# Four tokens to a partition, a second layer one step behind, and scatters two experts behind

## The chip, the core and the metric

The kernel runs on one core of a Trainium2 chip. The core has a matrix engine (TensorE, PE in the profile, with PEld for its weight loads), three other compute engines (VectorE or DVE, ScalarE or ACT, GpSimd or POOL), a queue engine (SyncE or SP) and 16 DMA engines. The metric is the device time of one execution in microseconds (us); lower is better.

## The reference

```python
x = x + xattn(ctx_512, layernorm(x), W0, ..., b0, W1, ..., b1)     # two graph attention layers
x = x + ffn(layernorm(x), gate_w, gate_up_proj, down_proj, shared_gate_w, shared_up_w, shared_down_w)

def gat_layer(x, adj, W, a_self, a_neigh, b):
    feat = einsum('nf,hfo->hno', x, W)
    e = leaky_relu(attn_self[:, :, None] + attn_neigh[:, None, :])
    e = e + MASK_VAL * (1.0 - adj)[None, :, :]                      # adj is layernorm(x)
    out = einsum('hnm,hmo->hno', softmax(e), feat) + b[:, None, :]
    return elu(out)

def ffn(x, ...):                                                    # 64 experts, 6 a token, 128 slots
    scores = softmax(xf @ gate_w.T); topk_w, topk_idx = top_k(scores, 6)
    hid = silu(g) * u; eo = (hid @ down_proj) * weight              # for each expert, on its tokens
    return scatter_add(eo) + silu(xf @ shared_gate_w.T) * (xf @ shared_up_w.T) @ shared_down_w.T
```

x is 4 batches of 512 tokens of 512 numbers, the context 4 x 512 x 128. All is float32. The mask term is so large that each token attends to one node only, the one with the largest layernorm value. So the kernel computes an attention layer as product, bias and elu on all nodes, and applies the two attention steps as one lookup: node of node, then a gather of feature rows. A flag worked out from bounds on the inputs sends other inputs to a general path, which does not run here.

## The kernel before

Token n of a batch sits in partition n % 128 of tile n // 128: 4 tiles of 128 tokens to a batch, 16 in all.

**The first stretch** is a loop over 16 steps, one for each tile (n = 4b + t). On PE a step holds one column block of the first layer of the next batch (`first_layer`, L577), the four products of the second layer of this tile (`second_layer`, L587) and two transposes of shared weights in steps 4 to 11 (`weight_turn`, L560), which start only when all four loads of `raw_in` have landed. ACT and DVE follow in the same order. On DVE a step also holds `elu2` of the tile before (L992) and the search for the largest x (`largest`). SP stores each feature tile to DRAM (`store_feat`, L302). POOL stores the four node columns of a batch (`store_node`, L402, 4 bytes to a descriptor), looks up node of node (L408), gathers the feature rows (`pick`, L420), adds them to x (`add`, L429) and finishes the scale of the normalisation (`scale`). DVE takes the moments in `moments` (L1026), and ACT writes the normalised rows (`norm`, L856: it reads x with a step of four numbers and writes runs). PE transposes them (`xn_turn`, L567).

**The second stretch** is the routing of the four batches, in an order written out by hand on each engine: gate product (`gate`, L601: the tokens are the standing operand, the 64 gate columns stream), choice of six (`choose`), positions in the experts (`place`), one-hot columns (`split`, DVE), and products that turn them into a list of tokens for each expert (`invert`, `collect`). Ten units of the shared part of batch 0 lie in between or behind: `half_up` is units 0 to 5 (L664) and `shared_down` units 6 to 9 (L678). Six of them stand between the routing steps and four behind the last of them. ACT takes part with `silu` (L881), which waits for a unit.

**The third stretch** is the loop over 64 experts. PE: the product with `gu_w` (L785), the transposes of the next expert's gathered rows (L765), a unit of the shared part in some steps (30 units over 52 experts), the product with `dn_w` of the expert before (L773). DVE scales the result into one of `YB` = 8 buffers y (L1215). POOL runs one queue in this order:

```python
for e in range(E):
    scatter(e, 0)
    scatter(e, 1)
    if e + GX < E:
        gather(e + GX)
    if e + 1 < E and shared_before(e + 1) > shared_before(e):
        for h in range(2):
            pool.wait_ge(half_added[h], 16 * (e + 1))
        add_shared(shared_before(e + 1))
```

`scatter(e, h)` (L507) adds half of every row to the output in DRAM. It waits for y of expert e and for the landing of the same half of expert e - 1, so the 64 scatters of a half are a chain. `gather(e)` (L514) fills one of `GX` = 6 buffers and waits for y of expert e - 6. `add_shared` (L498) adds a batch's shared part to the output. It comes behind the scatters of experts 19, 36 and 53, waits until they have landed, and the next scatter waits for it.

Of the kernel before, what the change touches and what calls it, by code (L numbers as in the profile page):

```python
# [37 lines left out]
YB = 8  # L38
EXP_FLOOR = -87.336
# [27 lines left out]
def allocate(nc, ctx, k):  # L67
# [14 lines left out]
    k.eighth = sb("eighth", [P, P], F16)  # L82
    k.pick_a = sb("pick_a", [P, (2 * SLO - 1) * SHI], F16)
# [7 lines left out]
def main_block(nc, k, a):  # L91
# [3 lines left out]
    with ExitStack() as ctx:  # L95
# [7 lines left out]
        with ExitStack() as early:  # L103
            def er(name, shape, dt=F32):
                return early.enter_context(nc.sbuf_tensor(name, shape, dt))

            gate_raw = er("gate_raw", [E, D])
            raw = er("raw", [P, 2 * SC, D])
            raw_down = er("raw_down", [P, KC, SI])
            absw = er("absw", [P, KC + 1, H * O], F16)  # L110
            square = er("square", [P, 2, D], F16)
# [22 lines left out]
        spare2 = sb("spare2", [P, E])  # L134
        sg = sb("sg", [P, 2, N])
# [3 lines left out]
        with ExitStack() as first:  # L139
# [4 lines left out]
            w1 = at("w1", [P, KC, H * O])  # L144
# [14 lines left out]
            at("behind_nodes", [P, 3, 256])  # L159
# [23 lines left out]
            wts = at("wts", [P, 2, TB, E])  # L183
# [16 lines left out]
        w0_in, b0_in, small_in, w1_in, raw_in = (sem(s) for s in ("w0_in", "b0_in", "small_in", "w1_in", "raw_in"))  # L200
# [3 lines left out]
        node_stored = [sem(f"node_stored{j}") for j in range(2)]  # L204
# [60 lines left out]
        order += [("xn", n) for n in range(NT)]  # L265
# [19 lines left out]

        ahead = [4, 6, 8, 9, 10, 11, 12, 13, 14, 15, 16] + [NT] * 6

        with nc.Block() as block:
            @block.sync
            def _(sp):  # L290
                def load_nodes(b):
                    sp.dma_start(nodes[:, b * TB:(b + 1) * TB, :],
                                 a["ctx"][b * N:(b + 1) * N, :].rearrange("(t p) f -> p t f", p=P)).then_inc(nodes_in[b], 16)
# [5 lines left out]
                def store_feat(b):  # L299
                    for t in range(TB):  # L300
                        sp.wait_ge(z2_ready, b * TB + t + 1)
                        sp.dma_start(a[f"feat_dram{b}"][t * P:(t + 1) * P, :], feat[:, t, :]).then_inc(feat_out[t], 16)  # L302

                def store_x2(b):
                    sp.wait_ge(x2_ready, (b + 1) * TB)
                    sp.dma_start(a["out"][b * N:(b + 1) * N, :].rearrange("(t p) d -> p t d", p=P),
                                 k.x[:, b * TB:(b + 1) * TB, :]).then_inc(x2_out, 16)

                def load_expert(e):
# [4 lines left out]
                    for j in range(2):  # L314
# [4 lines left out]
                             a["W0"].rearrange("h f o -> f h o")).then_inc(w0_in, 16)  # L319
                load_nodes(1)  # L320
                load_x(0)
                for c in range(KC):
                    sp.dma_start(w1[:, c, :].rearrange("f (h o) -> f h o", h=H),
                                 a["W1"][:, c * P:(c + 1) * P, :].rearrange("h f o -> f h o")).then_inc(w1_in, 16)
                sp.dma_start(b1bc[:], a["b1"].rearrange("h o -> (h o)").rearrange("(u d) -> u d", u=1)
                             .broadcast_to([P, H * O])).then_inc(w1_in, 16)
                load_x(1)
                load_nodes(2)
                load_x(2)
                load_nodes(3)  # L330
                sp.dma_start(gate_raw[:], a["gate_w"]).then_inc(raw_in, 16)
                load_x(3)
                sp.dma_start(raw[:, 0:SC, :], a["sh_gate"].rearrange("(s p) d -> p s d", p=P)).then_inc(raw_in, 16)
                sp.dma_start(raw[:, SC:2 * SC, :], a["sh_up"].rearrange("(s p) d -> p s d", p=P)).then_inc(raw_in, 16)
                sp.dma_start(raw_down[:], a["sh_down"].rearrange("(c p) s -> p c s", p=P)).then_inc(raw_in, 16)
                for j, name in enumerate(("a_self0", "a_neigh0", "a_self1", "a_neigh1", "b0")):
                    sp.dma_start(small[:, j, :], a[name]).then_inc(small_in, 16)
                store_feat(0)
                store_feat(1)
                store_feat(2)  # L340
                store_feat(3)
# [13 lines left out]
                sp.dma_start(a["out"][0:N, :].rearrange("(t p) d -> p t d", p=P), k.x[:, 0:TB, :]).then_inc(x3_out, 16)  # L355
# [5 lines left out]
            def _(pool):  # L361
                counted = [0]

                def count(ins):
# [11 lines left out]
                nc.gpsimd.iota(token_i[:], pattern=[[P, NT]], base=1, channel_multiplier=1)  # L376
                nc.gpsimd.memset(k.tri[:], 1.0 / SLO)
                nc.gpsimd.memset(k.eighth[:], 1.0 / SLO)
                nc.gpsimd.memset(k.pick_a[:], 0.0)
# [4 lines left out]
                nc.gpsimd.affine_select(out=k.tri[:], in_=k.tri[:], compare_op=ALU.is_gt, fill=0.0,  # L384
                                        base=0, pattern=[[1, P]], channel_multiplier=-1)
# [14 lines left out]
                def store_node(b):  # L400
                    pool.wait_ge(node_ready, b + 1)
                    pool.dma_start(a[f"node_dram{b}"].rearrange("(t p) u -> p (t u)", p=P),  # L402
                                   node[:, b * TB:(b + 1) * TB], allow_slow_non_contiguous=True).then_inc(node_stored[b % 2], 16)

                def node_of_node(b):
                    pool.wait_ge(node_stored[b % 2], 16 * (b // 2 + 1))
# [45 lines left out]
                def weigh(b):  # L452
# [11 lines left out]
                    pool.dma_start(a["rows_dram"][b * N:(b + 1) * N, D:ROW].rearrange("(t p) r -> p t r", p=P),  # L464
                                   wts[:, b % 2]).then_inc(wts_out[b % 2], 16)
# [1092 lines left out]
```

## Time and profile before

| | |
|---|---|
| median of 3 runs | 702.58 us (699.43 to 702.7) |
| the profiled execution | 701.51 us, of which the span is 699.7 us |
| TensorE busy, mean granted clock | 584.8 us (84%), 0.92 |
| GpSimd busy | 346.3 us (49%) |
| DVE, ACT busy | 229.2 us, 172.9 us |
| first transposes of the expert loop | 210.97 us |
| last scatter issued | 687.48 us |
| moved by DMA | 141.46 MB, 202 GB/s over the span |

The span runs from the first to the last instruction. The 1.8 us by which the execution is longer lie around it. A granted clock of 1.0 is 2.4 GHz, and 0.5 is 1.2 GHz.

### The profile page before, as it was taken

The page shows a single profiled execution, that of the slowest core. Times are in us where ns is not written, and L with a number is a line of the kernel's source. Part 1 is how long each engine was busy: PE and PEld are TensorE (multiplying, and loading weights), DVE is VectorE, ACT ScalarE, POOL GpSimd, SP SyncE. Part 2 cuts the span into 40 slices and gives each one's busy share as a digit, 9 for nine tenths or more (in the row PEclk, how much of TensorE's full clock was granted, in tenths as well). Part 3 has the DMA queues.
Part 4 walks back from the last instruction along what each step waited for, and adds up shares of the span by engine and source line. Part 5 has one row for each costly group of instructions (what it writes and reads, how often), then busy time and mean ns, then how long its engine had stood idle before and what let it go on. Part 6 is the DMA issues. An engine that isn't in the chain of part 4 may idle for free. (4 is left out here: it accounts for less than half of the span.)

```text
span 699.7 us, 6458 instructions
## 1 busy us (share of the span) xinstructions
PE 584.8 (84%) x2035; PEld 314.2 (45%) x2035; DVE 229.2 (33%) x575; ACT 172.9 (25%) x352; POOL 346.3 (49%) x299
## 2 busy tenths in 40 slices
PE   5998928776889999999998799997969999873950
PEld 2444414544534555555554455553535545441520
DVE  3865632865742322222222122221212222220220
ACT  4666742475101111112111111210101111110100
POOL 1134755262140656565642756556256565653662
PEclk9999959878989999999999899998989999897895
DMA  8945334569332989999889799988989999898752
GB/s 229 250 130 92 51 84 155 207 201 292 109 109 81 264 236 251 278 240 276 252 241 259 157 274 257 274 249 182 225 205 267 233 275 243 249 285 174 158 61 35
DMA packets 78170, 141.46 MB, mean 202 GB/s; under 512 B 14576, under 2 KB 33520, under 8 KB 78128
## 3 DMA queue, kind: packets, MB, share of 16 engines
q1 hardware_dynamic: 48240, 93.22, 43.7%
q0 software_dynamic: 27248, 43.55, 32.4%
q10 hardware_dynamic: 2640, 4.20, 1.7%
q8 instruction: 18, 0.29, 0.2%
q14 instruction: 24, 0.20, 0.1%
HBM read 107.89 MB, written 33.04 MB: 201 GB/s over the span
## 5 line engine op out<-in xcount | busy, mean ns | idle before, releaser
L507 POOL DMA_INDIRECT out<-y,half_at x128 | 200.6, 1567 | 191.6 <-DMA out<-y,half_at 59.2
L785 PE MATMUL bank<-gu_w,gxT 128*128 128x384 f32 x512 | 177.4, 490 | 0.8 <-ACT gxT L957 0.8
L773 PE MATMUL bank<-dn_w,hidT 96*128 96x512 f32 x256 | 125.4, 613 | 0.9 <-DVE hidT L1232 0.9
L1215 DVE TENSOR_SCALAR y<-bank,gx 128x512 f32<-128x512 f32 x64 | 48.0, 751 | 225.5 <-PE bank L773 202.4
L785 PEld LDWEIGHTS bank<-gu_w,gxT 128*128 128x128 f32 x512 | 93.2, 192 | 52.6 <-issue 2.5
L664 PE MATMUL bank<-xnT,upT 128*128 128x512 f32 x192 | 94.1, 636 | 0.0
L965 ACT ACTIVATE eg<-bank 128x192 f32<-128x192 f32 x64 | 21.1, 330 | 288.8 <-PE bank L785 288.8
L514 POOL DMA_INDIRECT gx<-rows_dram,table x64 | 64.3, 1005 | 21.7 <-issue 17.1
L1227 DVE TENSOR_TENSOR hid<-bank,eg 128x192 f32<-128x192 f32 x64 | 31.7, 496 | 130.7 <-ACT eg L965 130.7
L765 PE MATMUL bank<-ident,gx 128*128 128x128 f32 x256 | 41.3, 287 | 36.0 <-DMA gx<-rows_dram,table 35.8
L773 PEld LDWEIGHTS bank<-dn_w,hidT 96*128 96x128 f32 x256 | 47.5, 197 | 48.3 <-issue 46.8
L587 PE MATMUL bank<-w,h1T 128*128 128x512 f32 x128 | 59.8, 613 | 0.0
L765 PEld LDWEIGHTS bank<-ident,gx 128*128 128x128 f32 x256 | 32.6, 147 | 59.6 <-DMA gx<-rows_dram,table 43.1
L957 ACT ACTIVATE gxT<-bank 128x512 f32<-128x512 f32 x64 | 38.2, 597 | 70.0 <-PE bank L765 64.4
L664 PEld LDWEIGHTS bank<-xnT,upT 128*128 128x128 f32 x192 | 37.9, 208 | 39.0 <-issue 39.0
L678 PE MATMUL bank<-downT,shid 128*128 128x512 f32 x96 | 45.1, 612 | 0.4 <-DVE shid L1123 0.4
L567 PE MATMUL bank<-ident,rows 128*128 128x128 f32 x64 | 15.3, 401 | 29.9 <-ACT xnT L806 17.2
L587 PEld LDWEIGHTS bank<-w,h1T 128*128 128x128 f32 x128 | 24.8, 198 | 29.8 <-issue 29.0
L797 PEld LDWEIGHTS bank<-ident,hid 128*96 128x96 f32 x128 | 16.6, 130 | 36.5 <-issue 35.7
L408 POOL DMA_INDIRECT node<-node_dram,node x16 | 16.8, 1047 | 26.5 <-DMA node_dram<-node 22.5
L567 PEld LDWEIGHTS bank<-ident,rows 128*128 128x128 f32 x64 | 11.1, 206 | 34.3 <-ACT rows L856 22.7
L1232 DVE COPY hidT<-bank 96x256 f32<-96x256 f32 x64 | 26.2, 410 | 0.5 <-PE bank L797 0.5
(167 smaller groups left out, 465.1 us busy)
## 6 DMA issues: line engine op xcount, KB each, us to landing
gu_w<-in_gate_up SPq DMA_DIRECT2D x128, 384.0 KB, 4.6
dn_w<-in_down SPq DMA_DIRECT2D x128, 192.0 KB, 5.8
x<-in_x SPq DMA_DIRECT2D x4, 1024.0 KB, 9.0
feat_dram<-feat SPq DMA_DIRECT2D x16, 256.0 KB, 3.8
rows_dram<-rows ACTq DMA_DIRECT2D x4, 1024.0 KB, 4.8
out<-x SPq DMA_DIRECT2D x4, 1024.0 KB, 5.7
out<-x POOLq DMA_DIRECT2D x3, 1024.0 KB, 11.7
out<-y,half_at POOLq DMA_INDIRECT x128, 5.4
```

The costliest lines, as they stand in the source:

```text
L507: pool.indirect_dma_start(halves, bass.IndirectOffsetOnAxis(ap=half_at[:, h, e:e + 1], axis=0), y[:, e % YB, h * (D // 2):(h + 1) * (D // ...
L514: pool.indirect_dma_start(gx[:, e % GX, :], None, a["rows_dram"][:, :], bass.IndirectOffsetOnAxis(ap=table[:, e:e + 1], axis=0)).then_inc( ...
L567: last = nc.tensor.transpose(to[:, c * P:(c + 1) * P], rows[:, (n // TB) % 2, n % TB, c * P:(c + 1) * P], k.ident[:])
L587: last = nc.tensor.matmul(L2[t % 2][:], h1T[:, b % 2, c, t * P:(t + 1) * P], w1[:, c, :], start=(c == 0), stop=(c == KC - 1))
L664: last = nc.tensor.matmul(UP[g][:], k.upT[:, c, g * SI + s * P:g * SI + (s + 1) * P], xnT[:, c, b * N:(b + 1) * N], start=(c == 0), stop=( ...
L678: last = nc.tensor.matmul(UP[t % 2][:], shid[b % 2][:, s, t * P:(t + 1) * P], k.downT[:, s, :], start=(s == 0), stop=(s == SC - 1))
L765: last = nc.tensor.transpose(GT[e % 2][:, c * P:(c + 1) * P], gx[:, e % GX, c * P:(c + 1) * P], k.ident[:])
L773: last = nc.tensor.matmul(DN[:], hidT[:, e % 2, j, :], dn_w[:, e % U, j, :], start=(j == 0), stop=(j == 1))
L785: last = nc.tensor.matmul(GU[e % 2][:, 0:2 * I], gxT[:, e % 2, c, :], gu_w[:, e % U, c, :], start=(c == 0), stop=(c == KC - 1))
L957: nc.scalar.activation(gxT[:, e % 2, :, :].rearrange("p c q -> p (c q)"), GT[e % 2][:], ACT.Copy).then_inc(gxT_ready, 1)
L1215: nc.vector.tensor_scalar(y[:, e % YB, :], DN[:], gx[:, e % GX, D + e:D + e + 1], None, ALU.mult).then_inc(y_ready, 1)
L1227: nc.vector.tensor_tensor(hid[:].rearrange("s j p -> s p j"), GU[e % 2][:, I:2 * I].rearrange("s (p j) -> s p j", j=2), eg[:].rearrange("s ...
```

## The change

- A partition holds four consecutive tokens (`(p t)` in place of `(t p)` in all loads and stores of x, context, nodes, features and rows). A descriptor covers 8 KB of x in place of 2 KB, and 16 bytes of node numbers in place of 4. `place` needs three more products for the order of tokens, with two new constant matrices, `strict` and `upto`.
- `W1` is loaded by one DMA (runs of 1 KB) right behind `W0`, and `b1` and `b0` from ACT's queue. `x` of batch 0 comes behind `W1`, and the four loads of `raw_in` come ahead of `x` of batch 3. The transposes of shared weights begin in step 2 instead of 4.
- `store_node` goes from POOL's queue to SP's.
- On ACT the second layer lags PE by a step, and on DVE `elu2` lags two steps. Four normalisations, transposes and the gate product of batch 0, and two or four of batch 1, move into the steps.
- `gate` holds the gate columns still and streams 512 tokens. ACT copies the 64 x 512 result, and four transposes bring it back (`turn_logits`).
- `norm` reads x in order and writes with a step of 128 numbers.
- The power of `sumsq` on POOL, which stood ahead of `scale(2)`, goes to the end of the routing. `silu(0, 1)` goes behind the last `norm`.
- Two units (4 and 5) go behind the last routing step, so that six units stand there.
- In the expert loop the gather comes first, and the scatters lag two experts.

```diff
+LAG = 2
-                 a["x"][b].rearrange("(t p) d -> p t d", p=P)).then_inc(x_in[b], 16)
+                 a["x"][b].rearrange("(p t) d -> p t d", t=TB)).then_inc(x_in[b], 16)
 def wt_of(n):
-    return range(2 * (n - TB), min(2 * (n - TB) + 2, len(wt))) if TB <= n < 3 * TB else range(0)
+    return range(2 * (n - 2), min(2 * (n - 2) + 2, len(wt))) if 2 <= n < 2 + (len(wt) + 1) // 2 else ()
+xn_of = {10: (0,), 11: (1, 2), 12: (3,), 15: (4, 5)}
 # POOL, first and second stretch
-store_node(0)
 node_of_node(0)
-store_node(1)
 node_of_node(1)
-store_node(2)
 pick(0)
 add(0)
 node_of_node(2)
 scale(0)
-store_node(3)
 pick(1)
...
 add(2)
-pool.wait_ge(sq_ready, 1)
-nc.gpsimd.tensor_tensor(sumsq[:], sumsq[:], k.mhalf[:], ALU.pow).then_inc(sq_rstd, 1)
+count_seen(0)
 scale(2)
-count_seen(0)
 pick(3)
...
 weigh(2)
+pool.wait_ge(sq_ready, 1)
+nc.gpsimd.tensor_tensor(sumsq[:], sumsq[:], k.mhalf[:], ALU.pow).then_inc(sq_rstd, 1)
 weigh(3)
 # POOL, expert loop
-for e in range(E):
-    scatter(e, 0)
-    scatter(e, 1)
+for e in range(E + LAG):
     if e + GX < E:
         gather(e + GX)
-    if e + 1 < E and shared_before(e + 1) > shared_before(e):
+    if e < LAG:
+        continue
+    d = e - LAG
+    scatter(d, 0)
+    scatter(d, 1)
+    if d + 1 < E and shared_before(d + 1) > shared_before(d):
         for h in range(2):
-            pool.wait_ge(half_added[h], 16 * (e + 1))
-        add_shared(shared_before(e + 1))
+            pool.wait_ge(half_added[h], 16 * (d + 1))
+        add_shared(shared_before(d + 1))
 # PE
 def gate(b):
     pe.wait_ge(turn_sb, turn[("xn", b * TB + TB - 1)] + 1)
+    to = begin_turn(("lg", b))
+    for c in range(KC):
+        last = nc.tensor.matmul(to[0:E, :], k.gateT[:, c, :], xnT[:, c, b * N:(b + 1) * N],
+                                start=(c == 0), stop=(c == KC - 1))
+    last.then_inc(turn_done, 1)
+def turn_logits(b):
+    pe.wait_ge(turn_sb, turn[("lg", b)] + 1)
...
     for t in range(TB):
-        for c in range(KC):
-            last = nc.tensor.matmul(POS[:, t * E:(t + 1) * E], xnT[:, c, n * P:(n + 1) * P], k.gateT[:, c, :],
-                                    start=(c == 0), stop=(c == KC - 1))
+        last = nc.tensor.transpose(POS[:, t * E:(t + 1) * E], lgT[:, t * P:(t + 1) * P], k.ident[0:E, 0:E])
     last.then_inc(logits, 1)
 # PE behind the steps
+xn_turn(6)
+xn_turn(7)
 place(0)
+gate(1)
 unit(0)
-gate(1)
+turn_logits(1)
 invert(0)
+place(1)
 for t in range(TB):
     xn_turn(2 * TB + t)
+gate(2)
+turn_logits(2)
 unit(1)
-place(1)
-gate(2)
 invert(1)
-unit(2)
 invert_rest()
...
 place(2)
+for t in range(TB):
+    xn_turn(3 * TB + t)
 gate(3)
+turn_logits(3)
+unit(2)
 invert(2)
-unit(4)
 place(3)
-unit(5)
+unit(3)
 invert(3)
...
-for u in range(6, units):
+for u in range(4, units):
     unit(u)
 # ACT
-nc.scalar.activation(rows[:, b % 2, t, :].rearrange("q (c p) -> q c p", c=KC),
-                     k.x[:, n, :].rearrange("q (p c) -> q c p", c=KC), ACT.Identity,
+nc.scalar.activation(rows[:, b % 2, t, :].rearrange("q (c p) -> q p c", c=KC),
+                     k.x[:, n, :].rearrange("q (p c) -> q p c", c=KC), ACT.Identity,
                      scale=k.rstd[:, n:n + 1], bias=shift[:, b % 2, t:t + 1]).then_inc(xn_ready, 1)
```

## Rows read from the trace of the kernel before

**Rows 1.** Windows: length, busy PE, PEld, DVE, ACT, POOL, PEclk, DMA share, GB/s
```profile
...
17.40:87.10 69.70, 64.28 (x180) 29.76 (x178) 47.67 (x97) 47.25 (x108) 29.86 (x30) 0.98 0.59 131
87.10:103.60 16.50, 2.27 (x9) 1.43 (x8) 6.53 (x14) 8.21 (x13) 9.52 (x10) 0.58 0.41 83
103.60:120.10 16.50, 16.45 (x64) 10.00 (x64) 2.58 (x4) 3.88 (x7) 9.72 (x10) 0.91 0.50 169
120.10:197.20 77.10, 53.51 (x364) 36.20 (x364) 54.67 (x229) 34.37 (x66) 24.60 (x32) 0.83 0.60 185
197.20:211.00 13.80, 13.36 (x37) 5.80 (x36) 4.15 (x13) 0.00 (x0) 5.82 (x6) 0.81 0.46 133
...
412.70:626.00 213.30, 197.98 (x635) 105.77 (x634) 48.98 (x93) 34.38 (x71) 120.25 (x88) 0.95 0.94 246
...
```

**Rows 2.** PE timeline, first stretch: start, us, line, [idle before, releaser]
```profile
...
17.45 3.60 PE L587 MATMUL bank<-w,h1T 128*128 128x512 f32 x8
...
21.74 3.60 PE L587 MATMUL bank<-w,h1T 128*128 128x512 f32 x8
...
40.45 0.45 PE L560 MATMUL bank<-ident,gate_raw 64*128 64x64 f32 x2
...
103.64 1.94 PE L567 MATMUL bank<-ident,rows 128*128 128x128 f32 x8 [11.27 <-ACT xnT L806]
...
109.49 3.68 PE L601 MATMUL bank<-gateT,xnT 128*128 128x64 f32 x32
...
```

**Rows 3.** POOL timeline of the first two stretches
```profile
...
68.38 4.96 POOL L429 TENSOR_TENSOR x<-x,picked 128x512 f32<-128x512 f32 x4 [7.07 <-DMA picked<-feat_dram,node]
...
136.33 2.94 POOL L484 TENSOR_TENSOR sumsq<-sumsq,mhalf 128x16 f32<-128x16 f32 x1 [20.29 <-DVE sumsq L1155]
...
```

**Rows 4.** ACT timeline of the second stretch
```profile
...
164.53 0.60 ACT L881 ACTIVATE sg<-bank 128x512 f32<-128x512 f32 x1 [10.27 <-PE bank L664]
...
```

**Rows 5.** Waits, whole span: us in total, times, longest
```profile
...
POOL out L507 <- DMA out<-y,half_at: 59.2, 31, 4.0
...
PE bank L765 <- DMA gx<-rows_dram,table: 35.8, 9, 12.0
...
```

**Rows 6.** POOL timeline: first scatters of experts 19, 20, 24, 36, 54, 63
```profile
...
358.51 1.57 POOL L507 DMA_INDIRECT out<-y,half_at  x1 [1.51 <-DMA out<-y,half_at]
...
380.63 1.63 POOL L507 DMA_INDIRECT out<-y,half_at  x1 [11.12 <-DMA out<-x]
...
405.70 1.58 POOL L507 DMA_INDIRECT out<-y,half_at  x1 [2.96 <-DMA out<-y,half_at]
...
488.36 1.58 POOL L507 DMA_INDIRECT out<-y,half_at  x1 [0.30 <-issue]
...
639.14 1.64 POOL L507 DMA_INDIRECT out<-y,half_at  x1 [10.91 <-DMA out<-x]
...
685.60 1.55 POOL L507 DMA_INDIRECT out<-y,half_at  x1 [1.07 <-issue]
...
```

**Rows 7.** DVE timeline: y of experts 21, 24 and 36
```profile
...
366.75 0.75 DVE L1215 TENSOR_SCALAR y<-bank,gx 128x512 f32<-128x512 f32 x1 [4.74 <-PE bank L773]
...
396.75 0.75 DVE L1215 TENSOR_SCALAR y<-bank,gx 128x512 f32<-128x512 f32 x1 [12.99 <-PE bank L773]
...
473.78 0.75 DVE L1215 TENSOR_SCALAR y<-bank,gx 128x512 f32<-128x512 f32 x1 [1.30 <-PE bank L773]
...
```

**Rows 8.** Landing of scatters issued in 400 to 450 us
```profile
...
DMA to landing us min/median/max: 3.8/5.8/7.7
```

**Rows 9.** Landing of scatters issued in 662 to 690 us
```profile
...
DMA to landing us min/median/max: 3.6/3.8/4.0
```

**Rows 10.** Groups by line and shape, ACT, 60 to 200 us
```profile
...
L856 ACT ACTIVATE rows<-x,shift,rstd 128x512 f32<-128x512 f32 x16 | 19.4, 1288 | 9.7 <-POOL shift L438 9.7
...
```

**Rows 11.** Groups by line, whole page: busy us, mean ns
```profile
...
L1227 DVE TENSOR_TENSOR hid<-bank,eg 128x192 f32<-128x192 f32 x64 | 31.7, 496 | 130.7 <-ACT eg L965 130.7
...
L957 ACT ACTIVATE gxT<-bank 128x512 f32<-128x512 f32 x64 | 38.2, 597 | 70.0 <-PE bank L765 64.4
...
```

More of the change, by code:

```diff
@@ L203, in main_block @@
         node2_in = [sem(f"node2_in{j}") for j in range(2)]
[L204 removed]
+        node_stored = [sem(f"node_stored{b}") for b in range(B)]
         feat_out = [sem(f"feat_out{t}") for t in range(TB)]
@@ L264, in main_block @@
             order += [("wt", j) for j in wt_of(n)]
-        order += [("xn", n) for n in range(NT)]
+            order += [("xn", m) for m in xn_of.get(n, ())]
+            if n == 13:
+                order.append(("lg", 0))
+        order += [("xn", 6), ("xn", 7), ("lg", 1)]
+        order += [("xn", m) for m in range(2 * TB, 3 * TB)] + [("lg", 2)]
+        order += [("xn", m) for m in range(3 * TB, 4 * TB)] + [("lg", 3)]
         turn = {what: at_ for at_, what in enumerate(order)}
@@ L897, in _ @@
                 copy_nodes(1)
-                for n in range(NT):
+                for n in range(NT + 1):
                     b, t = n // TB, n % TB
@@ new lines, in _ @@
+                    if n == 10:
+                        norm(1)
+                        norm(2)
+                    if n == 11:
+                        norm(3)
+                    if n == 12:
+                        nc.scalar.activation(nodes[:], nodes[:], ACT.Abs).then_inc(abs_nodes, 1)
+                    if n == 13:
+                        store_rows(0)
+                    if n in (14, 15):
+                        norm(2 * n - 24)
+                        norm(2 * n - 23)
+                copy_xn(6)
@@ L935, in _, with turned @@
+                copy_xn(7)
+                copy_logits(1)
+                store_rows(1)
+                gate_exp(0)
+                def turned(b):
+                    for t in range(TB):
+                        copy_xn(b * TB + t)
+                    copy_logits(b)
+                    store_rows(b)
+                for t in range(TB):
+                    norm(2 * TB + t)
                 turned(2)
+                gate_exp(1)
+                act.wait_ge(squared, NT)
                 silu(0, 0)
-                gate_exp(1)
@@ L938, in _ @@
-                silu(0, 1)
-                norm(3)
+                for t in range(TB):
+                    norm(3 * TB + t)
                 turned(3)
                 gate_exp(2)
+                silu(0, 1)
+                act.wait_ge(small_in, 80)
+                for j in range(4):
+                    nc.scalar.activation(small[:, j, :], small[:, j, :], ACT.Abs,
+                                         accum_out=bounds[:, 3 + j:4 + j]).then_inc(abs_small, 1)
+                nc.scalar.activation(small[:, 4, :], small[:, 4, :], ACT.Abs).then_inc(abs_small, 1)
@@ L1130, in _ @@
                     first_layer(0, c)
-                for t in range(TB):
-                    largest(t)
+                    largest(c)
                 for n in range(NT):
-                    second_layer(n)
+                    b, t = n // TB, n % TB
+                    if n >= 2:
+                        elu2(n - 2)
+                    if b + 1 < B:
+                        first_layer(b + 1, t)
+                    for j in range(ahead[n], ahead[n + 1]):
+                        largest(j)
                     if n == 2 * TB - 2:
@@ L1148, in _ @@
                                                 AX_X, ALU.max).then_inc(abs_nodes, 1)
[L1149 removed]
+                    if n == 15:
+                        choose(0)
+                    second_layer(n)
+                elu2(NT - 2)
                 elu2(NT - 1)
[L1151 removed]
+                split_high(0)
+                split_low(0)
+                choose(1)
                 moments(2)
[L1153 to L1159 removed]
+                split_high(1)
+                split_low(1)
+                add_last()
                 split_rest()
```

249 lines of the change are left out of this document (126 added, 123 removed).

## The prediction, made before the changed kernel ran

> **What bounds the kernel now.** I first cut the span into stretches by windows [rows 1]: where TensorE (PE) is near full, only fewer products help, and elsewhere the order of waits decides. Then I read the timelines of PE, POOL and ACT in the first two stretches [rows 2 to 4], and in the expert loop the waits and the spacing of scatters and results [rows 5 to 9].
>
> The first stretch is the sixteen steps, from 17.4 to 120.1 us. PE is busy 64.28 us up to 87.1, then 2.27 us in a hole of 16.5 us, then 16.45 us [rows 1]: 83.0 us of work in 102.7, so 19.7 us idle. The reader is to see that the hole is one loop of waits. The transposes at 103.64 waited 11.27 us for ACT's copies [rows 2]. ACT stood in order behind a second-layer step, that behind DVE's moments of batch 1, and these behind POOL's addition. POOL itself had been late since batch 0, whose addition began at 68.38 after 7.07 us for its gathers [rows 3]. These gathers follow a node store with 4 bytes to a descriptor on the same queue.
>
> The second stretch is the routing, 120.1 to 197.2. PE is busy 53.51 us of 77.1, at a granted clock of 0.83, between the levels of 1.2 and 2.4 GHz [rows 1]. It is a chain from batch to batch with two waits by order alone. POOL stood 20.29 us before the power of `sumsq`, with `scale(2)` and `pick(3)` queued behind it [rows 3]. ACT stood 10.27 us before a silu until a PE unit ended, with the last four normalisations behind it [rows 4]. From 197.2 to 211.0 PE is full with units 6 to 9.
>
> In the loop PE looks like the bound, 197.98 us of 213.3 in 412.7 to 626 [rows 1], and its idle time is mostly for gathers, 35.8 us in nine waits [rows 5]. But the end of the span is the last scatter, so the scatters need their own reading. The first halves of experts 24 and 36 go at 405.70 and 488.36 [rows 6]: 6.89 us a pair. The results y of the same experts come at 396.75 and 473.78 [rows 7]: 6.42 us each. The scatters are slower than PE there, and fall from 9 to 15 us behind. What they wait for is the landing of the scatter before, 59.2 us in 31 waits [rows 5]. A landing takes 5.8 us while weights stream in, and 3.8 us when they have stopped [rows 8, 9]. So in most of the loop the chain of scatters is as tight a bound as PE, and at the end it alone is.
>
> **The change, part by part. First stretch.** Work stays about the same. Gone are the order waits: node stores leave POOL's queue, so the gathers of a batch have nothing ahead of them. The first addition should end near 61 us instead of 73.3 (68.38 + 4.96) [rows 3]. The moments of batches 0 and 1 then find their data when DVE comes to them in steps 8 and 13, and the transposes of batch 0 fill gaps in steps 10 to 12. A node store on SP stands behind the loads and lands near 40 us at the earliest. That is late, but the first gathers need the features of step 3 anyway, near 50 us. So I count it as nothing; if that cover is gone, it costs a few us of POOL. The start of step 0, at 17.45 [rows 2], I leave: W1 comes sooner, but x of batch 0 comes later, and DVE searches it between the first-layer steps. With all idle time gone the steps would end at 17.4 + 83.0 = 100.4 us.
>
> One new wait: the transposes of shared weights begin in step 2 and need all of `raw_in`. A step is 4.29 us (17.45 to 21.74), so step 2 ends near 30.3. The first such transposes ran at 40.45 [rows 2], with all loads landed. In the new order only the last 1 MB of x, of some 9 MB in all, comes behind, which is 4 to 5 us of the first 40. So they land near 36 us and PE waits 5.5 us; behind it stand all later steps. The sum is 100.4 + 5.5 = 105.9, less about 1 us of slow clock in the hole and behind it (granted 0.58 and 0.91) [rows 1]: 105 against 120.1, so **-15 us**. Bounds: -8, if ACT's longer queue (normalisations, copies and abs in the steps) keeps half the idle time, and -19.7, if nothing is left.
>
> `gate` at 3.68 us for 32 small products [rows 2] becomes 8 of 512 columns. Eight such products of the second layer take 3.60 us [rows 2]. Then come a copy (0.6 us, as L957 [rows 11]) and four transposes. That is no gain in work and about 1 us more latency for each batch; it is in the next sum, as are the three extra products of `place`.
>
> **Second stretch.** `pick(3)` no longer waits for `sumsq`, but now for `moments(2)`, which DVE does behind `choose(1)`. I step through the order from the end of the steps: two transposes, `place(0)`, `gate(1)`, a unit and `turn_logits(1)` are 12 us, `choose(1)` and the moments 7 us, the scale 1.3. So `pick(3)` comes 21 us behind the steps, where it was 22. The silu wait is another matter: without the 10.27 us [rows 4] the last `norm` comes 10 to 12 us earlier, and the rest of the chain with it. I take -11 for the end of the routing. Then two more units stand behind it. The four took 13.8 us with other small work [rows 1], and two more of eight products of 512 columns are 3.4 us each: +6.9, less 2 us for a better clock. The stretch gives -11 + 5 = **-6 us** (bounds 0 and -14), and the expert loop begins near 190 us.
>
> How fast `norm` is also bears on this chain. Reading with a hop of four numbers it takes 1288 ns [rows 10], where a plain copy of the same size takes 597 ns [rows 11]. The new form reads in order and writes with a hop of 128. The nearest row is `hid`, DVE's write with a hop of 96: 496 ns for 192 numbers, 2.6 ns each [rows 11], which is no faster for each number than 1288 for 512. I take no gain; at 597 ns the four of the last batch would give back 2.8 us. On this the Trainium skill (SBUF — State Buffer, "Door 1: The DMA port swizzle") says that memory comes in lines of 16 bytes and each access to a new line pays. By that rule the new write pays as the old read did, and the sum has 0 in place of -2.8.
>
> **Expert loop.** PE's work is the same 30 units and 64 experts. The gather of expert e + 6 now goes as soon as y(e) is there, and PE may run seven experts ahead of the scatters instead of five. The price is that scatter d waits for y(d + 2). At expert 19 the scatter went at 358.51, and y(21) came at 366.75 [rows 6, 7]. The new place is y(21) and a gather of 1.3 us, 368.0: 9.5 us later. From there the pace is that of landings, 6.89 us, not PE's 6.42, so PE cannot give the delay back. The three additions of the shared part keep their price: 358.51 to 380.63 is 22.1 us where a pair is 6.9 [rows 6]. What comes back is at the tail: nine pairs from 639.14 to 685.60 took 5.16 us each [rows 6], still with weights and gathers among them. With PE further ahead more of them land in 3.8 us [rows 9], and I take -2.5. The loop gives 9.5 - 2.5 = **+7 us** (bounds -12 and +24, by the rivals below). Covered is PE's wait for gathers: less of it, and no gain, since the scatters end last.
>
> **Sum.** 701.51 (the profiled execution: 699.7 and 1.8 around it) - 15 - 6 + 7 = 687.5. The median of the runs is 1.1 us above the profiled one, so 688.5 there. Less than 0.5%, 3.5 us, cannot be told from no change.
>
> **Rivals.**
> *The gathers set the loop* (0.20). PE's stops for gathers, 35.8 us [rows 5], go, and with an even load landings fit PE's pace. Over 33 pairs 6.89 - 6.42 is 15.5 us less, with the +7 a loop of -8 to -9, and 2 more from the tail: 702.6 - 21 - 10.5 = 671. For it: scatters waited for y in the first third. Against it: they lag 9 to 15 us later on.
> *ACT's queue takes the waits* (0.18). Normalisations, copies and the lagging second layer stand in one order, and one wait for POOL's scale holds all. The first two stretches give -8 in all: 702.6 - 8 + 7 = 701.6. For it: ACT's waits set the hole before. Against it: ACT is busy only 47.25 of 69.7 us [rows 1].
> *The scatters slow down* (0.12). PE no longer pauses, weights stream without a break, and landings grow from 5.8 us towards the 7.7 seen [rows 8]. At 7.6 us a pair instead of 6.9 over 34 pairs it is +24: 712. It ends above 706.1 from 0.55 us a pair on. Against it: the DMA share is 0.94 already [rows 1], with little left to add.
>
> **How the numbers follow.** My forecast has 0.50, with its own range 678 to 698. The rivals at 671, 701.6 and 712 have 0.20, 0.18 and 0.12. The range 670 to 703 takes in the first two and leaves out the third and the rim of the first. Faster: 0.50 + 0.20 and a third of ACT's case, 0.76. Same: 0.11. Slower: 0.13.
>
> **What would show it.** Right: second-layer products without a hole up to 105 us, with one wait of 4 to 7 us behind step 2; no wait over 5 us on ACT before a silu; the loop's first transposes near 190; scatter 19 some 14 us behind its y; fewer and shorter waits for gathers on PE; and the distance from y(63) to the last scatter well over 10 us. Wrong: a loop start later than 200, PE waiting for x or nodes in the first 20 us, or a pair spacing in the middle of the loop that is not 6.7 to 7.1 us.

## The result, and the profile after

The changed kernel is slower, by less than 1%: 708.55 us, the median of 14 runs, where the kernel before took 703.78 in the 14 runs beside them. The ratio is 1.0083 (95% interval 1.0048 to 1.0119), some 6 us. Forecast were 688.5 us and a range that ended at 703. The profiled execution took 706.33 us with a span of 703.9.

| us from the span's start | before | after | forecast |
|---|---|---|---|
| the sixteen steps end | 120.1 | 105.7 | 105 |
| the routing ends (products for the list) | 197.2 | 185.2 | 172 |
| first transposes of the loop | 211.0 | 208.0 | 190 |
| y of expert 63 | 675.6 | 664.9 | |
| last scatter begins | 687.5 | 692.1 | 673 |

The windows of the changed kernel, with the columns of [rows 1], show which part held:

```profile
17.40:105.70 88.30, 83.70 (x234) 41.54 (x235) 63.57 (x116) 62.62 (x125) 45.71 (x44) 0.96 0.42 137
105.70:186.40 80.70, 50.24 (x304) 26.51 (x303) 56.69 (x234) 31.89 (x74) 26.27 (x34) 0.78 0.53 181
186.40:208.00 21.60, 20.82 (x50) 8.76 (x48) 3.61 (x11) 0.60 (x1) 5.84 (x6) 0.86 0.29 83
```

In the first, PE is busy 83.70 of 88.30 us: the hole of [rows 1] is gone. In the second it is idle 30 us, and its clock is lower than the 0.83 of before. The third is PE full with most of the work behind the routing. From the last routing product at 185.2 to the loop it is 22.8 us with six units, where it was 13.8 with four. So 14.4 us were won ahead of 105.7 and 11.4 lost again by 208. From there to the last scatter it is 484.1 us, before 476.5: 7.6 more.

Why the routing is slow stands in DVE's timeline (start, us, line, and in brackets the idle time before and what ended it):

```profile
101.83 0.69 DVE L1068 TENSOR_TENSOR s<-bank,b1bc 128x512 f32<-128x512 f32 x1 [3.33 <-PE bank L607]
102.44 5.08 DVE L1044 SCALAR_TENSOR_TENSOR feat<-ex,feat 128x512 f32<-128x512 f32 x1
107.44 0.41 DVE L1109 TENSOR_REDUCE topc<-bank 128x4 f32<-128x256 f32 x1
...
126.94 2.46 DVE L1074 BATCH_NORM_STATS2 bn<-x 128x6 f32<-128x512 f32 x4
...
147.37 0.18 DVE L1164 RECIPROCAL rsum<-esum 128x4 f32<-128x4 f32 x1 [11.63 <-ACT ex L905]
147.46 1.28 DVE L1097 TENSOR_TENSOR x<-x,picked 128x512 f32<-128x512 f32 x2
...
172.64 0.18 DVE L1164 RECIPROCAL rsum<-esum 128x4 f32<-128x4 f32 x1 [5.12 <-ACT ex L905]
```

Three things are to be seen. `choose(0)` (L1109) begins at 107.44, behind an instruction that took 5.08 us where it takes 0.68 elsewhere. The moments of batch 2 run at 126.94, behind `choose(1)`. And DVE stands 11.63 us before a reciprocal that only POOL needs, with the addition of batch 3 and its moments queued behind. It waits for exponentials that ACT has behind the copy of the next batch's logits, which waits for a gate product:

```profile
145.62 0.59 ACT L835 ACTIVATE lgT<-bank 64x512 f32<-64x512 f32 x1 [6.41 <-PE bank L616]
...
155.33 4.36 ACT L890 ACTIVATE rows<-x,shift,rstd 128x512 f32<-128x512 f32 x4 [6.08 <-POOL shift L457]
```

That product, on PE, ran partly at the lower clock. The granted clock was 0.71 in the first of these lines, 0.57 in the second and 1.00 in the third, where the same eight products take 3.65 us:

```profile
114.30 5.10 PE L616 MATMUL bank<-xnT,gateT 128*64 128x512 f32 x8 [2.41 <-ACT xnT L835]
...
139.26 6.26 PE L616 MATMUL bank<-xnT,gateT 128*64 128x512 f32 x8 [0.69 <-ACT xnT L835]
...
165.88 3.65 PE L616 MATMUL bank<-xnT,gateT 128*64 128x512 f32 x8 [0.69 <-ACT xnT L835]
```

In the loop, first scatters of experts 0, 19, 20 and 63 and the second of 63, on POOL, against [rows 6]:

```profile
237.46 1.63 POOL L522 DMA_INDIRECT out<-y,half_at  x1 [0.31 <-issue]
...
370.69 1.57 POOL L522 DMA_INDIRECT out<-y,half_at  x1 [2.34 <-DMA out<-y,half_at]
...
389.11 1.62 POOL L522 DMA_INDIRECT out<-y,half_at  x1 [8.37 <-DMA out<-x]
...
689.49 1.56 POOL L522 DMA_INDIRECT out<-y,half_at  x1 [0.42 <-issue]
692.07 1.56 POOL L522 DMA_INDIRECT out<-y,half_at  x1 [1.03 <-DMA out<-y,half_at]
```

y of expert 63 is there at 664.93, 10.6 us earlier than before, and its last scatter goes 27.1 us behind it (before 11.9). The engines are ahead and the chain of scatters is late. Waits over the whole span:

```profile
POOL out L522 <- DMA out<-y,half_at: 81.7, 37, 3.8
...
PE bank L794 <- DMA gx<-rows_dram,table: 27.2, 13, 5.2
DVE rsum L1164 <- ACT ex L905: 18.2, 3, 11.6
```

The wait for landings grew from 59.2 [rows 5] to 81.7 us; PE's for gathers fell from 35.8 to 27.2, to no use. The first of the two sums is no measure of the loss, though: `best` below, the fastest kernel together with `best2`, has 80.7 us of the same wait.

### The profile page after: what moved, and what is told of

It is laid out like the page before. It is cut to its first block and busy times, and to the rows that moved or that the text cites. A ratio compares the mean times of both kernels' runs of the same rounds, so it can differ in the third digit from the quotient of the medians.

```text
span 703.9 us, 6338 instructions
## 1 busy us (share of the span) xinstructions
PE 589.6 (84%) x1967; PEld 307.9 (44%) x1967; DVE 235.4 (33%) x575; ACT 173.2 (25%) x356; POOL 344.1 (49%) x299
## 5 line engine op out<-in xcount | busy, mean ns | idle before, releaser
L522 POOL DMA_INDIRECT out<-y,half_at x128 | 200.7, 1568 | 166.0 <-DMA out<-y,half_at 81.7
L802 PE MATMUL bank<-dn_w,hidT 96*128 96x512 f32 x256 | 127.5, 622 | 0.9 <-DVE hidT L1308 0.9
L692 PE MATMUL bank<-xnT,upT 128*128 128x512 f32 x192 | 90.4, 616 | 0.0
L794 PE MATMUL bank<-ident,gx 128*128 128x128 f32 x256 | 41.6, 288 | 27.2 <-DMA gx<-rows_dram,table 27.2
L692 PEld LDWEIGHTS bank<-xnT,upT 128*128 128x128 f32 x192 | 36.2, 199 | 38.2 <-issue 38.0
L706 PE MATMUL bank<-downT,shid 128*128 128x512 f32 x96 | 43.5, 594 | 0.8 <-DVE shid L1187 0.8
L595 PE MATMUL bank<-ctxT,w 128*128 128x512 f32 x32 | 20.6, 737 | 7.1 <-ACT ctxT L835 3.6
L826 PE MATMUL bank<-ident,hid 128*96 128x128 f32 x128 | 25.6, 282 | 0.6 <-DVE hid L1303 0.6
```

The costliest lines, as they stand in the source:

```text
L522: pool.indirect_dma_start(halves, bass.IndirectOffsetOnAxis(ap=half_at[:, h, e:e + 1], axis=0), y[:, e % YB, h * (D // 2):(h + 1) * (D // ...
L692: last = nc.tensor.matmul(UP[g][:], k.upT[:, c, g * SI + s * P:g * SI + (s + 1) * P], xnT[:, c, b * N:(b + 1) * N], start=(c == 0), stop=( ...
L706: last = nc.tensor.matmul(UP[t % 2][:], shid[b % 2][:, s, t * P:(t + 1) * P], k.downT[:, s, :], start=(s == 0), stop=(s == SC - 1))
L794: last = nc.tensor.transpose(GT[e % 2][:, c * P:(c + 1) * P], gx[:, e % GX, c * P:(c + 1) * P], k.ident[:])
L802: last = nc.tensor.matmul(DN[:], hidT[:, e % 2, j, :], dn_w[:, e % U, j, :], start=(j == 0), stop=(j == 1))
L826: last = nc.tensor.transpose(HT[0:IH, j * P:(j + 1) * P], hid[:, j, :], k.ident[:])
```

## The experiments

Each experiment was timed in five rounds with the kernel before. Differences are taken between ratios to before, since the kernels ran in several sessions, at about 7.0 us for 1%. The interval of a ratio is between 0.3 and 1.0% wide on either side, so a difference to the changed kernel is uncertain by 3 to 6 us, for step_nolag by 7 (worked out from both intervals). "Loop" is the length from the first transposes to the last scatter in the one profile of each.

| kernel | ratio, 95% interval | against changed | loop |
|---|---|---|---|
| before | 1 | | 476.5 |
| changed | 1.0083, 1.0048 to 1.0119 | | 484.1 |
| lag0 | 0.9882, 0.9855 to 0.9909 | -14.1 us | 473.6 |
| lag1 | 0.9988, 0.9949 to 1.0026 | -6.7 | 480.4 |
| lag2_only | 1.0212, 1.0184 to 1.0240 | (+14.9 on before) | 485.9 |
| order | 0.9824, 0.9795 to 0.9852 | -18.2 | 487.9 |
| moments | 0.9917, 0.9878 to 0.9956 | -11.7 | 488.3 |
| exps | 0.9973, 0.9931 to 1.0016 | -7.7 | 482.9 |
| gate_old | 0.9959, 0.9915 to 1.0003 | -8.7 | 488.3 |
| units | 0.9987, 0.9954 to 1.0021 | -6.7 | 489.7 |
| pool_store | 0.9996, 0.9947 to 1.0046 | -6.1 | 481.0 |
| step_nolag | 1.0197, 1.0100 to 1.0294 | +8.0 | 484.0 |
| best | 0.9668, 0.9612 to 0.9723 | -29.1 | 471.5 |
| best2 | 0.9673, 0.9600 to 0.9745 | -28.7 | 472.0 |

**The lag of the scatters: lag0, lag2_only, lag1.** The first puts the old loop back into the changed kernel, the second the new loop into the kernel before, the third sets the lag to one.

```diff
-for e in range(E + LAG):
-    if e + GX < E:
-        gather(e + GX)
...
-    d = e - LAG
-    scatter(d, 0)
-    scatter(d, 1)
+for e in range(E):
+    scatter(e, 0)
+    scatter(e, 1)
+    if e + GX < E:
+        gather(e + GX)
```

> The changed kernel with POOL's expert loop in the old order (scatter of e, then gather of e + 6, no lag); everything else as changed. Theory (the lag costs): the loop grew from 476.5 to 484.1 us because scatter d waits for y(d + 2) and the chain of landings never gives those 13 us of delay back; without the lag the kernel gains 6 to 9 us on the changed one, about 700.5 on the scale of its profile, and the first pair of experts 19 and 36 goes within 1 to 15 us of its y. Rival (the layout costs): the additions of the shared part and the gathers run against rows laid out four to a partition, and the lag is neutral because PE gets its gathers earlier; then lag 0 stands within 2 us of the changed kernel.

> The kernel before with nothing changed but POOL's expert loop: gather first, scatters two experts behind. Theory (the lag costs): 6 to 9 us slower than before, last scatter over 20 us behind y(63) where it was 12. Rival (the layout costs): within 2 us of before, since in the loop the layout, not the lag, made the difference.

> The changed kernel with a lag of one expert instead of two. Theory (each expert of lag delays the chain of scatters by one result): half of what the lag costs, 702 us, between 695.8 (no lag) and 708.6 (two). Rival (the order gather before scatter costs, whatever the lag): as the changed kernel, 707 or more.

Removing the lag gives 14.1 us, adding it to before costs 14.9, and one expert of lag costs half. The sizes are larger than the 6 to 9 us that the theory gave, in both directions alike (by the raw medians the first is 12.7), and the rival that layout makes the difference falls. The profiles agree: nine kernels with a lag of two have loops of 481.0 to 489.7 us (mean 485.8), four without it 471.5 to 476.5 (mean 473.4), the one with a lag of one 480.4. That is 12.4 us for the lag. A single pair gives less: 10.5 us shorter without it (lag0), 9.4 longer with it (lag2_only). Another 2.2 and 3.7 us of these two profiles lie ahead of the loop, where the two kernels differ in nothing from those they are held against, so a single profile is good to a few us only. In the profile of lag0 expert 0 scatters 1.6 us behind its y, not 15.6, and the last scatter starts 12.8 us behind y(63), not 27.1:

```profile
221.27 1.62 POOL L522 DMA_INDIRECT out<-y,half_at  x1 [28.24 <-DVE y L1288]
...
679.33 1.55 POOL L522 DMA_INDIRECT out<-y,half_at  x1 [0.43 <-issue]
```

**The order of the routing: order, moments, exps.** The second and third are the halves of the first.

```diff
 # DVE
+moments(2)
 split_high(0)
 split_low(0)
 choose(1)
-moments(2)
...
-split_low(1)            # ends with the reciprocal of batch 1
-add_last()
+split_low(1)
+add_last()
+sums(1)                 # the reciprocal, a function of its own
 # ACT, for each batch b from 1
+gate_exp(b - 1)
 copy_logits(b)
 store_rows(b)
-gate_exp(b - 1)
```

> The changed kernel with three moves in the routing and no other edit: the moments of batch 2 on DVE ahead of the first split instead of behind the choice of batch 1; on ACT the exponentials of batch b ahead of the copy of the logits of batch b + 1; on DVE the reciprocal of the sums of batch 1 behind the addition of batch 3. Theory (the order of queues costs): pick(3) goes near 119 us instead of 132, DVE's waits of 11.6 and 5.1 us for the exponentials go, the collection of the list ends near 168 instead of 185, and the kernel is 12 to 17 us faster than the changed one: some 691. Rival (the gate product and its copy cost): the chain from transposes over a slow gate product of 5 to 6 us, copy and transposes sets the batches; then the end of the routing moves by less than 5 us.

> The changed kernel with only the moments of batch 2 ahead of the first split on DVE. Theory A (the wait of DVE for the exponentials decides): pick(3) goes near 119 us, but DVE still stands before the reciprocal until the exponentials behind the copy of the logits of batch 2, which itself comes some 8 us earlier: 6 to 9 us faster than the changed kernel. Theory B (the place of pick(3) decides): most of the 15 us, 12 to 15. Theory C (neither matters alone): under 3 us.

> The changed kernel with only the exponentials ahead of the next copy of logits and the reciprocal behind the last addition. The picks of batch 3 land near 140 us and DVE's wait ended at 147.4, so at most 7 us can come from it while pick(3) stays at 132. Theory A: 5 to 8 us faster than the changed kernel. Theory B (pick(3) decides): under 3 us. Theory C (the gate product of batch 2, 6.3 us long, decides): under 3 us too, with DVE idle for the logits instead.

`order` gains 18.2 us (15.0 by the raw medians, where 12 to 17 were expected); the halves give 11.7 and 7.7, which add up to it within the intervals. `exps` alone is within the 5 to 8 of its theory A. With `moments` alone `pick(3)` begins at 119.07 instead of 132.26; its gain lies between what theories A and B said, so both the place of the moments and the wait for the exponentials counted. In `order` DVE's waits of 11.63 and 5.12 us are 0 and 0.72, and PE shows the end of the routing at 171.3 and the loop at 192.55, where the forecast had put them (172 and 190):

```profile
170.91 0.41 PE L675 MATMUL bank<-cross,pick_a 128*128 128x64 f16 x8 [0.87 <-DVE cross L1179]
...
192.55 0.60 PE L794 MATMUL bank<-ident,gx 128*128 128x128 f32 x4
```

**The form of the gate product: gate_old.**

```diff
-last = nc.tensor.matmul(to[0:E, :], k.gateT[:, c, :], xnT[:, c, b * N:(b + 1) * N],
+last = nc.tensor.matmul(POS[:, t * E:(t + 1) * E], xnT[:, c, n * P:(n + 1) * P], k.gateT[:, c, :],
...
-gate(1)
 unit(0)
-turn_logits(1)
+gate(1)
```

> The changed kernel with the gate product as before: the tokens stand still and the weights stream, 32 products of 64 columns straight into the logits, no copy and no transposes of logits; unit 0 ahead of it again. Theory (order of queues, not the form of the product, held the routing): the gate takes 3.7 us instead of 5 to 6 and saves the copy, but the exponentials no longer stand behind a copy of logits either, so the wait of 11.6 us shrinks for that reason: 5 to 9 us faster than the changed kernel. Rival (the new form gives PE a faster product that a slow clock hides): under 2 us.

It gains 8.7 us, within the expected 5 to 9, but not by the product of batch 2: in the old form that took even longer, 7.09 us at a granted clock of 0.50.

```profile
135.79 7.09 PE L619 MATMUL bank<-gateT,xnT 128*128 128x64 f32 x32 [0.69 <-ACT xnT L822]
...
136.87 0.18 DVE L1142 RECIPROCAL rsum<-esum 128x4 f32<-128x4 f32 x1 [4.58 <-ACT ex L887]
```

With no copy of logits ahead of the exponentials, DVE waits 4.58 us instead of 11.63. `exps` gets nearly all of the 8.7 us with the new form, so in the kernel's time the form shows no share of its own. In the profiles it is less clear: the routing ends at 175.7 in gate_old and at 180.6 in exps, but gate_old's loop is 5.4 us longer. What the form is worth in the routing stays open.

**Six units or four: units.** Units 4 and 5 go back into the routing, and the silu and the product of that pair move ahead with them (not shown).

```diff
 invert(1)
+unit(2)
 invert_rest()
...
-unit(2)
+unit(3)
 invert(2)
+unit(4)
 place(3)
-unit(3)
+unit(5)
 invert(3)
...
-for u in range(4, units):
+for u in range(6, units):
```

> The changed kernel with units 4 and 5 back inside the routing, as before (unit 2 behind the first inversion, 3 to 5 around place(3)), and the silu and product of unit pair 1 moved ahead of them. Theory (the units behind the routing cost): the tail from the list to the first loop transposes falls from 23 to 14 us and the routing end moves by at most 2, since PE is idle 2 to 6 us at a time there: 5 to 8 us faster than the changed kernel. Rival (PE's time is the same wherever it stands): the units delay the products that the routing waits for, and the gain is under 2 us.

The tail falls from 22.8 to 13.5 us, but the routing ends 5.3 us later, at 190.5, and the loop begins 4.1 earlier. The gain by the ratio is 6.7 us, by the raw medians (708.55 and 704.87) 3.7; the one profile, with a loop 5.6 us longer, shows none (707.73 against 706.33). So the tail behaved as the theory said and the end of the routing as the rival said, and the net gain is known only to some 3 us.

**The first stretch: step_nolag, pool_store.** The first does ACT's and DVE's share of a step in the step again, the second moves the four node stores back to POOL's queue in the new layout.

```diff
 # step_nolag, ACT
-    if n:
-        second_layer((n - 1) // TB, (n - 1) % TB)
+    second_layer(b, t)
...
 # step_nolag, DVE
-    if n >= 2:
-        elu2(n - 2)
...
     second_layer(n)
+    if n:
+        elu2(n - 1)
 # pool_store, POOL
+store_node(0)
 node_of_node(0)
+store_node(1)
 node_of_node(1)
+store_node(2)
 pick(0)
...
 scale(0)
+store_node(3)
 pick(1)
```

> The changed kernel with the second layer's work on ACT and DVE in the same step as its product again, everything else as changed, normalisations and copies in the same steps too. Theory (the hole of 16.5 us came from late additions, not from the missing lag): the sixteen steps end 2 to 6 us later than 105.7 by the short waits of each step, with no hole: 3 to 5 us slower. Rival (without the lag one wait holds ACT's whole queue and the hole returns): the steps end at 115 or later.

> The changed kernel with the node stores back on POOL's queue, in the old places, but in the new layout (one run of 16 bytes to a partition). Theory (the queue was what made the additions late): the first addition starts 5 to 10 us later than 55.1 us, the moments of batch 0 and the steps behind them slip, and the kernel is 3 to 10 us slower than the changed one. Rival (the layout of the store did it, 4 bytes to a descriptor before): first addition within 2 us of 55.1 and no change in time.

Without the lag of a step the steps end 8.8 us later (114.5), more than the 2 to 6 of the theory and without the hole of the rival. ACT then stands at one step behind DVE, held while POOL adds, and a gap opens at nearly every step:

```profile
88.42 0.63 ACT L872 ACTIVATE ex<-s 128x512 f32<-128x512 f32 x1 [4.52 <-DVE s L1066]
```

For pool_store the rival was right: the first addition begins at 55.70, against 55.10 in the changed kernel, and the kernel is no slower. It is even faster by 0.9% in ratio. In its profile the loop starts 4.0 us earlier, 0.9 of them by an earlier W0, and is 3.1 us shorter, where its edit touches nothing; whether more than chance is in it stays open. So the queue did not matter. What made the first addition earlier than in [rows 3] was the layout of the store or the rest of the new order, that of the loads among it; these were not separated.

**All together: best, best2.** `best` is lag0, order and units in one; `best2` adds two moves.

```diff
 # DVE, step 15
-elu2(13)
 choose(0)
+elu2(13)
 # PE
 invert_rest()
+for t in range(TB):
+    xn_turn(3 * TB + t)
 collect(RFIN, cross2, ...)
 place(2)
-for t in range(TB):
-    xn_turn(3 * TB + t)
```

> The changed kernel with the old scatter order (no lag), the three moves in the routing, and units 4 and 5 back inside the routing. If the three act one behind the other, their gains on the changed kernel add up (12.7 + 15.0 + 3.7 us by the runs of each alone): 677 us. Rival (the expert loop takes it back): the loop is bound by its transfers, which do not start earlier than before when the routing ends earlier, as the loop of the run with the units back was 5.6 us longer than that of the changed kernel; then it is 684 or more.

> The best kernel so far with two more moves: the choice of batch 0 on DVE ahead of the scaled result of step 13 (which stood 5.08 us instead of 0.69 while POOL ran its addition), and the last four transposes of normalised tokens ahead of the collection on PE. Theory (that DVE instruction is held by POOL's addition, and the chain of choices starts behind it): choice 0 begins at 102.5 instead of 107.4 us, at least its first instruction, which reads PSUM, takes no longer than 0.42 us, and the kernel gains 3 to 6 us on the best one. Rival (any DVE instruction between SBUF tiles is held as long as POOL adds): the second or third instruction of the choice takes the 5 us instead, and the gain is under 2 us, from the transposes alone.

`best` took 679.4 us, 3.3% less than before (interval 2.8 to 3.9%) and near the 677 of the sum; its loop is not longer, so the rival falls. That sum was taken from raw medians. By the ratios the three gains add up to 39.0 us, and together they gave 29.1. Some 7 us of that difference can be noise (an estimate from the intervals); the rest may lie in the routing, where DVE waits 10.89 us for a unit that now stands behind four transposes and a gate product.

```profile
166.45 0.69 DVE L1188 TENSOR_TENSOR shid<-bank,sg 128x512 f32<-128x512 f32 x1 [10.89 <-PE bank L689]
```

`best2` takes that wait down to 2.12 us and starts its loop 7.2 us earlier, yet its ratio is the same within the intervals (its median is 676.22 beside a slower kernel before, 705.18). Its DVE timeline answers the question about the 5.08 us:

```profile
102.30 0.41 DVE L1107 TENSOR_REDUCE topc<-bank 128x4 f32<-128x256 f32 x1
102.75 0.42 DVE L1110 TENSOR_TENSOR below<-bank,topc 128x256 f32<-128x256 f32 x1
103.21 3.97 DVE L1113 TENSOR_SCALAR key<-below 128x256 f32<-128x256 f32 x1
```

Tiles named `bank` lie in PSUM, where PE writes its products, and the others shown lie in SBUF, the on-chip memory for all else. The two that read PSUM pass; the third, from SBUF to SBUF, takes 3.97 us in place of 0.29, to the end of POOL's addition. The rival was right on this point, though not for any DVE instruction, as the last section shows.

## Why the prediction was wrong, step by step

The three terms gave -14 us up to the last scatter, and it came 4.6 us later than before. Of the 18.6 us between the two, 17.4 lie in the second stretch.

**First stretch, -15: right in sum (-14.4), not in its parts.** The steps end at 105.7 and the first addition at 61.84 (forecast 61). The new wait of 5.5 us for `raw_in` did not come: the transposes at 33.21 found their weights. In its place the first step began 3.0 us later, at 20.50 against [rows 2], a cost that the forecast had left at nothing. The lag of a step, which the forecast did not price, was needed for it: 8.8 us.

**Second stretch, -6: this step failed; it was +11.4.** The forecast said that without the silu wait of [rows 4] "the last `norm` comes 10 to 12 us earlier, and the rest of the chain with it". The silu wait did go (the only long one, 13.63 us, comes at 193.39, behind the routing). But the last normalisations begin 49.6 us behind the steps, where they began 44.9 and the forecast had 34 (44.9 less 11). The first line is of the kernel before, the second `pick(3)` of the changed one:

```profile
165.03 4.85 ACT L856 ACTIVATE rows<-x,shift,rstd 128x512 f32<-128x512 f32 x4
...
132.26 1.02 POOL L439 DMA_INDIRECT picked<-feat_dram,node  x1 [0.65 <-issue]
```

Two links make up the 15.7 us. `pick(3)` came 26.6 us behind the steps, not 21. The forecast had seen that `moments(2)` stands behind `choose(1)`, but not that `choose(0)` would start 4.4 us late behind the held instruction at 102.44, nor that the gate product of batch 1 would take 5.10 us instead of 3.65. From `pick(3)` to the last normalisations it is 23.1 us, and 13 in the forecast. The forecast had no wait there, and the reciprocal before the last addition makes DVE wait 11.63 us for ACT, and ACT for PE's next gate product. This was readable from the order of the queues in the code. Behind the normalisations the chain was 2.3 us shorter than before, so the routing ended 13.4 us later than forecast. The runs price the remedies: taking the wait away is worth 7.7 us, and putting the moments first, which makes up for more than the 5.6 us of `pick(3)`, 11.7.

The last 4.0 us are the two more units behind the routing, put at +5. That tail grew by 9.0, as the two took 9.77 us, at a granted clock of 0.73, and not 6.9:

```profile
187.02 9.77 PE L692 MATMUL bank<-xnT,upT 128*128 128x512 f32 x16
```

With both remedies, in `order`, the stretch ends at 192.55 us, near the forecast, but in part by luck: `pick(3)` then comes 13.6 us behind the steps, earlier than the 21 of the forecast, and the tail is still 21.2 us long.

**Expert loop, +7: right in sum (+7.6), by luck: its errors cancel.** Scatter 19 went 20.3 us behind its y, forecast 14.6: measured from the loop's start it was 15.2 us late, not 9.5. The delay of two results is there from expert 0 and nothing of it is regained before expert 19, because landings pace the scatters in the first third as well: up to expert 19 a pair of scatters takes 7.01 us and a result 6.77. The lag costs 12 us in the loop and 14 by the ratios; the difference of 2 is within the uncertainty. The pace of the pairs between the shared additions, taken as unchanged, was slower: 7.04 us over the 32 pairs from 20 to 36 and from 37 to 53, and 6.73 before, which is +10.0. It is 6.79 with the lag alone (lag2_only) and 6.94 with the layout alone (lag0), and from 6.71 to 7.07 over all kernels with the new layout, so how much of it is chance, and why it is slower, is open. Against these stood savings priced too small. From scatter 19 to that of 20, with a shared addition between, it is 18.4 us and not 22.1; "keep their price" was wrong. The next two additions saved more, 6.4 and 4.5 us, so the three gave -14.6. The lag alone saves 1.7 us there (lag2_only), the layout alone 7.3 (lag0), though none of that from 19 to 20. The last nine pairs took 4.75 us each (5.16 in [rows 6]), -3.7 us in all and not -2.5. With 0.7 us more in the last pair the sum is 15.2 + 10.0 - 14.6 - 3.7 + 0.7 = 7.6.

**The rivals.** None came true as written. "ACT's queue takes the waits" (701.6) was nearest in mechanism: one queue did take them, but in the routing and through DVE. It would have moved the loop's start to 203; it was 208. "The scatters slow down" (712) was nearest in number and had a part in the loop: 0.3 us a pair between the additions, where it had put 0.7. Its limit of 0.55 us a pair should have read 0.52 ((706.1 - 688.5) / 34). Of the signs of being wrong the loop start later than 200 came, and the spacing from expert 24 to 36 was 7.11 us, just outside 6.7 to 7.1. The price of `norm` was right: 16 of them have a mean of 1262 ns, against 1288 in [rows 10] (the last four 1.09 us each, against 1.21).

```profile
L890 ACT ACTIVATE rows<-x,shift,rstd 128x512 f32<-128x512 f32 x16 | 18.4, 1262 | 16.3 <-POOL shift L457 16.3
```

Here the trace agrees with the rule of the Trainium skill cited in the prediction: a hop moved from the read to the write saves next to nothing.

## What to carry to other kernels

An instruction whose result is wanted late (here a reciprocal for POOL) should not stand in a queue ahead of work that is wanted soon; follow each wait of an engine through the queue of the engine that ends it. When the last link of a kernel is a chain of transfers that wait for one another, a delay put before its first member can stay to the end (here 12 of 14 us), even if it frees the engines. And when a forecast moves the start of a chain, step through the new order once more with every wait in it, not only through the wait that was removed.

## What the runs showed of the hardware

Some DVE instructions between SBUF tiles stand while POOL runs an addition: the one with two SBUF inputs took 5.08 us for 0.68 in the changed kernel, and a `TENSOR_SCALAR` of float32 3.97 for 0.29 in best2. DVE instructions that read PSUM took their 0.41 to 0.69 us beside the same additions. So did two that read one SBUF tile, `MAX8` and `FIND_INDEX8`, 0.68 us each beside POOL's additions of 57.66 to 61.84. How long the wait lasts differs: that of 5.08 us went on through all four additions in POOL's queue, one of 2.42 us in `order` only to the end of the second. First the line of the changed kernel, then that of order:

```profile
60.19 0.68 DVE L1053 FIND_INDEX8 top_ix<-top,x 128x8 uint32<-128x512 f32 x1
...
83.30 2.42 DVE L1036 SCALAR_TENSOR_TENSOR h1T<-ex,h1T 128x512 f32<-128x512 f32 x1 [1.97 <-ACT h1T L864]
```

POOL can be the one that waits, too; here DVE runs products between SBUF tiles:

```profile
179.73 3.53 POOL L475 TENSOR_TENSOR ex<-ex,sel 128x256 f32<-128x256 f32 x1
```

The same takes 0.68 us at 137.16, when DVE is idle. The Trainium skill (SBUF — State Buffer, "SBUF: two separate sides") describes the port pair that the two share as a lock held for a whole instruction. The traces agree that one engine waits and the other does not slow down (POOL's four additions took 4.97 us beside the held instruction, and 4.91 at 93.14 in the kernel before, when DVE was idle), and show that the wait can last through several instructions in a row.

The shared additions of 1 MB land faster with rows of four tokens to a partition. The median from issue to landing of the three is 8.2 us, and was 11.7 in the profile of before. The layout alone gives a part of it only: lag0, with the new layout and no lag, has 10.6. In before and lag2_only, with the old layout, the single additions took 9.2 to 14.1 us, in the changed kernel, lag0, lag1, order, best and best2 7.8 to 10.8. The last number of the line is the median in the changed kernel:

```profile
out<-x POOLq DMA_DIRECT2D x3, 1024.0 KB, 8.2
```
